# Edges 3 of a four-layer graph network: gathering rows of x W1x + b1 made one phase earlier, with the attribute term alone on TensorE

## The reference

```
in_e   = concat(x[src], edge_attr_32)                  # 64 + 32 features per edge
hid_k  = relu(in_e @ msg_w1[k] + msg_b1[k])            # k = 0, 1: two message layers of width 64
msg    = sum over k of (hid_k @ msg_w2[k] + msg_b2[k])
agg    = sum of msg over the edges of a node / (its number of edges + 1e-8)
x_new  = layernorm(x + relu(concat(x, agg) @ upd_w1 + upd_b1) @ upd_w2 + upd_b2)
```

## Time and profile before

| | us |
|---|---|
| median of 3 runs | 8994.63 (8992.92 to 8995.6) |
| profiled execution, its span from first to last instruction | 12212.0 |
| profiled execution minus median | 3217.4 |

### The profile page before, as it was taken

How to read it: one execution, slowest core, us unless ns; L and a number is a source line. 1 busy time by engine, 2 the same in 40 slices (tenths; PEclk the granted TensorE clock), 3 DMA queues, 4 the chain that set the end, 5 groups by cost and what they waited for, 6 DMA issues and landing times. The chain is left out here.

```text
span 12212.0 us, 65741 instructions
## 1 busy us (share of the span) xinstructions
PE 2780.2 (23%) x15715; PEld 2525.3 (21%) x15715; DVE 4710.0 (39%) x6608; ACT 3336.3 (27%) x4637; POOL 6789.5 (56%) x6997
## 2 busy tenths in 40 slices
PE   2000000011000000044444444444333332333333
PEld 1000000010000000034334333333232222322233
DVE  3455555555666666432222222222231111111113
ACT  0222222233222222132222222222242232232231
POOL 6666666657777777644444444444435544544543
PEclk6555555555555555577666667667655555555556
DMA  6232323312222222222222222222111211211121
GB/s 270 91 99 95 98 95 99 99 47 74 98 98 94 98 93 96 69 75 76 76 76 76 76 76 76 75 73 79 39 42 55 63 62 55 63 62 59 59 62 52
DMA packets 366486, 982.75 MB, mean 80 GB/s; under 512 B 163828, under 2 KB 173582, under 8 KB 351652
## 3 DMA queue, kind: packets, MB, share of 16 engines
q1 hardware_dynamic: 135572, 667.06, 14.4%
q0 software_dynamic: 224608, 290.88, 9.4%
q10 hardware_dynamic: 6192, 23.73, 0.5%
HBM read 582.50 MB, written 398.69 MB: 80 GB/s over the span
## 5 line engine op out<-in xcount | busy, mean ns | idle before, releaser
L771 POOL DMA_INDIRECT se<-x_table,edge_ix x1512 | 1428.3, 945 | 1867.2 <-PEq L1343 1397.1
L771 POOL DMA_INDIRECT comb<-x_table,edge_ix x1512 | 1428.8, 945 | 1468.3 <-DMA edge_ix<-in_src 1010.4
L771 POOL DMA_INDIRECT g<-x_table,edge_ix x1512 | 1585.4, 1049 | 512.2 <-issue 512.2
L771 POOL DMA_INDIRECT qv<-qv_table,edge_ix x1484 | 1406.5, 948 | 681.1 <-issue 445.6
L889 DVE TENSOR_TENSOR_SCAN edge_val<-edge_bank,edge_val 128x464 f32<-128x464 f32 (+1 forms) x715 | 687.4, 1031 | 2469.3 <-ACT edge_val L1597 2462.9
L1565 PE MATMUL h_ps<-w_hidden,edge_comb_t 97*128 97x128 f32 x3136 | 699.3, 394 | 1924.3 <-issue 964.5
L899 ACT ACTIVATE edge_sums<-edge_val 128x1904 f32<-128x1904 f32 (+3 forms) x219 | 1107.0, 5055 | 0.0
L1454 DVE TENSOR_TENSOR edge_product<-mk_ps,edge_q_now 128x256 f32<-128x256 f32 x392 | 166.4, 424 | 2364.2 <-ACT edge_msg L1393 2344.8
L1565 PEld LDWEIGHTS h_ps<-w_hidden,edge_comb_t 97*128 97x128 f32 x3136 | 613.2, 291 | 2000.2 <-ACT edge_comb_t L1592 1009.0
L1353 PE MATMUL mk_ps<-w_mk,edge_se_t 128*128 128x128 f32 x3136 | 545.9, 329 | 1659.7 <-issue 1412.0
L1353 PEld LDWEIGHTS mk_ps<-w_mk,edge_se_t 128*128 128x128 f32 x3136 | 483.1, 235 | 1709.1 <-issue 1424.3
(11 more groups left out here) (416 smaller groups left out, 9145.2 us busy)
## 6 DMA issues: line engine op xcount, KB each, us to landing
sums<-edge_sums SPq DMA_DIRECT2D x56, 1848.0 KB
sums<-edge_sums SPq DMA_DIRECT2D x55, 1792.0 KB, 6.6
sums<-edge_sums SPq DMA_DIRECT2D x56, 1008.0 KB
sums<-edge_sums SPq DMA_DIRECT2D x55, 924.0 KB, 3.7
edge_k<-k_edges SPq DMA_DIRECT2D x56, 896.0 KB
edge_bond<-in_edge_attr SPq DMA_DIRECT2D x56, 896.0 KB
edge_eh<-in_edge_attr SPq DMA_DIRECT2D x56, 896.0 KB
edge_qr<-in_edge_attr_n SPq DMA_DIRECT2D x56, 896.0 KB
```

What stands on the lines that cost most here:

```text
L771: e.indirect_dma_start(self.gather_into(u, j), None, self.gather_from, bass.IndirectOffsetOnAxis(ap=now[:, j:j + 1], axis=0))\
```

## The change

Nodes 2 multiplies each finished group of x by W1x, adds b1 and stores the 128 hidden values per node to a table; x itself is stored no longer. Edges 3 gathers rows of 128 floats from that table. The attributes come from the host with features on the partitions, so that TensorE makes their term with seven matmuls of 512 columns per chunk against a block-diagonal weight, straight into PSUM; VectorE adds that to the gathered rows in place, and ScalarE takes one Relu per chunk, with features and edges swapped, into `val`.

- Tables: `x_tables` loses its third table; `hidden_table` [n, 128] is new.
- Weights: `w3_hidden` gives way to `w3_x` [128 x 256] (W1x twice on the diagonal, for a pair of nodes; 4 loads in place of 4) and `w3_e` (W1e four times on the diagonal, in the place of `w_nodes`; zeroed by VectorE and loaded by eight small DMAs on SP at the start of Nodes 2). msg_b1 joins the broadcast parameters.
- Nodes 2: transposing and copying x is now done for all 15 groups. `times_next` has one PSUM bank for its products, the hidden values two.
- Edges 3: `rows_free` is given by ScalarE after the Relu. The lay-out of the last chunk but one moves from VectorE to ScalarE, that of the last chunk's first 20 columns moves behind the add of its last 8.
- `sync` gets a size, since the turned attributes of a chunk are one row of the reshaped array. Their bytes per chunk and partition are the same 3584.

```diff
@@ edge_phase_3
+        g = [ctx.enter_context(nc.sbuf_tensor(f"hidden{b}", [P, J, P], F32)) for b in (0, 1)]
+        ph = EdgePhase(p, 3, ctx, p.hidden_table, lambda b, j: g[b][:, j, :], quads)
+        ea_t = [ph.sb(f"ea_t{b}", [P, quads, P]) for b in (0, 1)]
+        e_banks = ph.ps("e_ps", [P, quads, QUAD * P])
...
         @block.tensor
             with e.Fori(0, ph.rounds) as i:
                 for b in (0, 1):
-                    e.wait_ge(joined, at(i, 2, b + 1))
-                    turn(i, b, 0)
...
+                    ph.wait_attrs(e, i, b, 1)
+                    e.wait_ge(added, at(i, 2, b + 1))
+                    for q in range(quads):
+                        last = e.matmul(e_banks[:, q, :], ea_t[b][:, q, :], p.w3_e, start=True, stop=True)
+                    last.then_inc(made, 1)
...
         @block.scalar
-            def chunk(i, b, before, last=False):
...
+            def light(i, b):
+                e.wait_ge(added, at(i, 2, b + 2))
+                e.activation(ph.val[b][:, :, 1:], g[b].rearrange("p j f -> p f j"), ACT.Relu).then_inc(taken, 1)
+                e.drain().then_inc(ph.rows_free[b], 1)
+            with e.Fori(0, ph.rounds - 1) as i:
+                for b in (0, 1):
+                    light(i, b)
+                    ph.lay_out(e, i, b)
...
         @block.vector
+            def add(i, b):
+                ph.wait_gathered(e, i, b)
+                e.wait_ge(made, at(i, 2, b + 1))
+                e.sem_inc(ph.attr_free[b], 1)
+                e.tensor_tensor(g[b][:, :, :], g[b][:, :, :], e_ps, ALU.add)
+                e.drain().then_inc(added, 1)
             with e.Fori(0, ph.rounds - 1) as i:
                 for b in (0, 1):
                     begin(i, b)
+                    add(i, b)
                     sum_up(i, b)
...
@@ node_phase_2
         @block.tensor
+            def multiply_next(g):
+                e.wait_ge(times_next.moved, g + 1)
+                after(e, taken, g)
+                turned = times_next.tile_t[g % 2]
+                for k in range(times_next.pairs(g)):
+                    last = e.matmul(hidden_ps[:, k, :], turned[:, k, :], p.w3_x[:, :], start=True, stop=True)
+                last.then_inc(made, 1)
                 if g < early:
...
...
         @block.vector
+            def take_hidden(g):
+                n = ph.sizes[g]
+                after(e, stored[g % outs], 16 * (g // outs))
+                e.wait_ge(made, g + 1)
+                e.tensor_tensor(hidden_out[g % outs][:, 0:n, :],
+                                hidden_ps.rearrange("p k (u f) -> p (k u) f", u=2)[:, 0:n, :],
+                                bcast(p.param["L3_gnn_msg_b1"][:, :], 1, n), ALU.add)
+                e.drain().then_inc(taken, 1)
             in_turn(groups,
...
+                    (20, take_hidden), per=4)
```

More of the change, by code:

```diff
@@ L1582, in _ @@
         def _(e):
-            e.sem_inc(moved, 2)
-            e.sem_inc(taken, 2)
-            for b in (0, 1):
-                e.activation(comb[b][:, :, K - 1:], p.ones[:, 0:J].unsqueeze(2), ACT.Copy)
-            def move(i, b, c):
-                n = b * quads + c
-                e.wait_ge(turned, at(i, per, n + 1))
-                e.wait_ge(multiplied, at(i, per, n + 1))
-                e.activation(comb_t[n % 2][:, :, :], t_ps[n % 2][0:K, :, :], ACT.Copy).then_inc(moved, 1)
-            def take(i, b, c, into):
-                n = b * quads + c
-                e.wait_ge(multiplied, at(i, per, n + 3))
-                e.activation(into, h_ps[n % 2][:, :, :].rearrange("p j f -> p f j"), ACT.Relu).then_inc(taken, 1)
@@ L1599, in chunk @@
-            def chunk(i, b, before, last=False):
-                e.wait_ge(ph.rows_free[b], at(i, 1, 1))
-                ph.wait_attrs(e, i, b, 1)
-                e.activation(comb[b][:, :, FD:K - 1], ea[b][:, :, :], ACT.Copy).then_inc(joined, 1)
-                e.drain().then_inc(ph.attr_free[b], 1)
-                move(i, b, 0)
-                for c in range(quads):
-                    if c + 1 < quads - 1:
-                        move(i, b, c + 1)
-                    into = ph.val[b][:, :, 1 + QUAD * c:1 + QUAD * (c + 1)]
-                    if last:
-                        more = 1 if QUAD * c >= ph.cut else 0
-                        e.wait_ge(opened, 1 + more)
-                        from_ = 1 + QUAD * c - (ph.cut if more else 0)
-                        into = ph.part(more)[:, :, from_:from_ + QUAD]
-                    take(i, b, c, into)
-                    if c + 1 == quads - 1:
-                        move(i, b, c + 1)
-                    if c == 3 and before:
-                        ph.lay_out(e, *before)
@@ L1626, in _ @@
+            i = ph.rounds - 1
+            light(i, 0)
+            ph.lay_out(e, i, 0)
+            for more in (0, 1):
+                now = ph.columns(more)
+                e.wait_ge(added, 2 * i + 3 + more)
+                e.activation(ph.part(more)[:, :, 1:], g[1][:, now, :].rearrange("p j f -> p f j"), ACT.Relu)\
+                    .then_inc(taken, 1)
             ph.lay_out_first(e)
@@ L1629, in _ @@
         def _(e):
+            e.sem_inc(added, 1)
             ph.clear_carries(e)
@@ L1660, in _ @@
                 ph.carry_part(e, i, more)
-                if more == 0:
-                    e.sem_inc(opened, 1)
-                e.wait_ge(taken, i * per + quads + now.stop // QUAD + 2)
+                for c in range(now.start // QUAD, now.stop // QUAD):
+                    ph.wait_part(e, i, 1, c)
+                e.tensor_tensor(g[1][:, now, :], g[1][:, now, :], e_ps[:, now, :], ALU.add)
+                e.drain().then_inc(added, 1)
+                if more:
+                    ph.lay_out_cut(e, e.tensor_copy)
+                e.wait_ge(taken, 2 * i + 2 + more)
                 for part in range(8):
@@ L2308, in _ @@
         def _(e):
+            e.memset(p.w3_e, 0.0)
+            e.drain().then_inc(w_zeroed, 1)
             times_w.clear(e)
```

136 lines of the change are left out of this document (59 added, 77 removed).

## The result

The changed kernel takes 9010.89 us in the median of 17 runs (9005.12 to 9015.53), the kernel before 8992.9 in 17 runs beside it (8988.34 to 8995.8): ratio 1.0021, 95% interval 1.0014 to 1.0028. That is 18 us more, where 27.5 were forecast. Beside later runs it was 1.0018 (1.0009 to 1.0027).

A forecast was written before the change was run, and what follows sets the result against it. The prediction took GpSimd's gather issue to bound nearly every stage, with recorded stalls due to recording. Its terms 0 + 0 + 0 + 20 + 3.5 + 3 + 1 = 27.5 on 8994.6 gave 9022 us, own range 8997 to 9050.

The forecast's parts named there:

- The budget: Whole kernel: 6958 gathers plus 653 us of GpSimd waits at stage ends leave 1.20 us a gather, 1.29 without waits.
- The rival with cheaper gathers: Edges 3: unrecorded gathers take 1.15 us, so the loop sets the pace and gets faster, 8852 us; chance 0.28.
- Steps 1 to 3: Edges 3: work removed, work added, and gathers of 512 B instead of 256, each worth 0.
- Step 4: Nodes 2: added matmuls and VectorE's bias add cost 1.1 us a group, 18 x 1.1 = 20 us.
- takes it in its gaps: Nodes 2: VectorE's added 1.1 us falls into the 1.3 us it waits per group, about 9000 us; chance 0.13.
- Step 5: Last group of Nodes 2: its store also waits for transpose, move, matmul and add, 3.5 us.
- Step 6: End of Edges 3: add, Relu, scans and lay-out of the last columns follow the last gathers, +3 us.
- Step 7: Setup: one larger memset and one more broadcast load, about 1 us.
- the add slows the gathers: Edges 3: VectorE's add onto gathered rows slows gathers, 1.2 us a chunk, 67 in all, 9089 us; chance 0.09.

The follow-up runs named there:

- more_product: The changed kernel with TensorE repeating two of the four hidden-value matmuls per group in Nodes 2; 11451.9 us on kind B, where the kernel before took 12258.38.
- take_on_scalar: The changed kernel with TensorE adding b1 in Edges 3 and ScalarE, not VectorE, copying hidden values in Nodes 2; 11687.9 us on kind B, ratio 0.9536.
- the copy kernel: The changed kernel with VectorE instead of ScalarE copying out the lay-out of every Edges 3 chunk; 9169.82 us on kind A, 11447.62 on kind B.

## Why the prediction was right, and where not

**The verdict** held: slower, 18 us against 27.5, inside the forecast's own range, and for the reason given, Nodes 2. It held narrowly. The prediction counts as slower what lies 18 us or more over the kernel before, and the medians are 17.99 apart; that the kernel got slower at all rests on the interval, 13 to 25 us.

**What bounds the kernel.** The conclusion, that GpSimd's issue sets nearly every stage at 1.25 us a gather, was right for the timed runs. The reason was wrong: "the stalls of the earlier trace rows belong to the recording". They belong to a kind of chip, on which every unrecorded run is as long. The profile and the median that I compared came, as far as the record shows, from different kinds. The budget was also off: 653 us at stage ends left 1.20 us for a gather; on kind A it is 1.25, and 8990.3 - 6958 x 1.249 leaves 300. The rival with cheaper gathers (0.28) stood only on that 653. The Trainium skill's "NOTIFIC — the notification-queue block", section 7.1, says that the trace path could throttle an engine; recording didn't do so here: the recorded span of before is 2.6 us under the median of the runs on kind A, and on kind B that of more_product is 2.5 under its own.

**Steps 1 to 3** (work removed from and added to Edges 3, wider rows; 0 each) held on kind A: the gathers stay at 0.94. On kind B they are worth some 800 us (12258 against 11452 for more_product, 796 of them in Edges 3). The forecast of the changed profile was 800 to 1000 us less, about 11300, and 35 to 39 a chunk with gathers of 945 ns. The profile that came is of kind A, at 9013.6, so as a forecast of it that was wrong. Kind B comes near it: 11449.4 in more_product, 763 less, and 38.7 a chunk, but with gathers of 1053 ns. The prediction names gathers of over 1 us as a sign of contention, and on kind B they came.

**Step 4** (18 x 1.1 = 20) has the right sum, and that is partly luck. The last scaling of x starts 31.6 us after the last gather before and 50.9 after, 19.4 more. But only eight steps bear VectorE's price, at 1.26 us each, 10.1 in all; 8.8 more come in the last five groups, where TensorE's hidden product stands in the chain. A second add, which 18 steps at 1.15 would have made 20.7, cost 13.2. The step took VectorE's 1.1 in place of TensorE's "up to 2.5" for all groups: right while the pipeline is full, wrong behind that. TensorE at 8.9 of the step was wrong too, it is busy 6.7. The rival "takes it in its gaps" fell: the gaps stay 1.4 us.

**Step 5** (3.5): from there to the first gather of Edges 3 it was 5.2 us and is 9.4, 4.2 more.

**Step 6** (+3) is the term that made the sum too high. Its own figures give 3.6 + 1.2 + 2.96 + 2.9 - 6.9 = 3.8 and leave out the Relu of the last 8 columns; the chain behind the last gather grew by 1.7. And the step named the lay-out of the last chunk but one nowhere, though the diff moves it from VectorE to ScalarE: that gave 3.1 of the 4.1 us that Edges 3 lost. Together -2.4 stands for +3. In the recorded executions the whole is 23.3 us; the rest, down to the 18 of the medians, is within what single executions differ.

**Step 7** (+1): 0.7 at the first gather of Edges 0.

The rival "the add slows the gathers" fell too. The 1049 ns of Edges 1 that spoke for it are kind B's; on kind A they are 944 with the same adds, and in take_on_scalar they are 944 on kind B with the add in Edges 3.

## What to carry to other kernels

Where a profile's span is far from the timed runs, record the same kernel again before reading anything from the difference. A loop paced by one engine gives back nothing for work removed from the others; look instead at the stage that takes the work in, and there at the stream whose busy time plus small gaps fills the step. Count apart the full steps of a pipeline and its last groups: there the chain from engine to engine sets the time, and work put ahead of something that the next group waits for costs most of its length (3.1 of 3.8 us here). Keep long SBUF-to-SBUF copies of VectorE out of phases that GpSimd's gathers pace.

## What the runs showed that I had not expected

The same kernel takes 8993 us on two chips and 12258 to 12273 on two others, and the change is worth +0.2% on the first and about -6.6% on the second, where more_product and the copy kernel stood for it. On kind A a gather costs the same 943 to 944 ns and 1.25 us of pace for 256 and 512 bytes a row; on kind B a phase with nothing to wait for ran at 1.39. A 3.4 us copy on VectorE stretches a gather from 0.94 to 3.93 us. Moving the take from VectorE to ScalarE shortened the full steps by 6 us in all, and the stage got no shorter. And TensorE's granted clock in Nodes 2 was 0.50 before and 0.83 with the added products, so that its busy time rose by only 0.8 us a group while the pipeline was full; over the last five groups the clock was 0.74.
